# Expert results of a mixture-of-experts layer: weighted when they leave PSUM and added in DRAM to four sums per token, in place of six stored rows per token

## The reference

```python
router_logits = x @ gate_w.T
probs = softmax(router_logits)                   # 64 experts
topk_w, topk_idx = top_k(probs, 6)               # K = 6
topk_w = topk_w / sum(topk_w)
combine = sum(one_hot(topk_idx, 64) * topk_w)
h = silu(einsum('th,eih->tei', x, experts_w1))   # I = 176
y = einsum('tei,ehi->teh', h, experts_w2)
routed_out = einsum('teh,te->th', y, combine)
shared_out = (silu(g) * u) @ shared_down.T       # g, u from x @ shared_gate_up.T
x = layernorm(x + routed_out + shared_out)
```

## Time and profile before

| | |
|---|---|
| runs | 1177.99, 1176.19, 1179.95 us; median 1177.99 us |
| profiled execution | 1182.11 us; its span 1180.3 us |
| PE busy | 937.1 us (79%) |
| DVE busy | 787.1 us (67%) |
| POOL busy | 555.0 us (47%) |
| ACT busy | 414.3 us (35%) |
| DMA | 197.06 MB, mean 167 GB/s |
| router stage | 366 to 664 us, about 9.1 us a tile |
| expert stage | 669 to 1066 us, 6.75 us a unit |
| end stage | 1067 to 1172 us, about 3 us a tile |

### The profile page before, as it was taken

The page is one execution under the profiler, slowest core; times in us unless marked ns, Lnnn a source line. Parts: engine busy times, 40 slices in busy tenths (PEclk is TensorE's granted clock), DMA queues, the critical chain, the costliest instruction groups (busy, mean ns, idle before and its releaser), DMA issues.

```text
span 1180.3 us, 32353 instructions
## 1 busy us (share of the span) xinstructions
PE 937.1 (79%) x8988; PEld 806.4 (68%) x8988; DVE 787.1 (67%) x2416; ACT 414.3 (35%) x1061; POOL 555.0 (47%) x780
## 2 busy tenths in 40 slices
PE   5699999997988888888888399999999999980000
PEld 4577777775767888788877288888888888870000
DVE  5477777774435677767766566766676766746995
ACT  2355655553213443444343023232232232231121
POOL 1022222222003777777777345656656656663553
PEclk9899999998988999999999599999999999995555
DMA  7445555552311333333324366777777777727994
GB/s 237 127 144 184 175 168 167 182 180 65 89 58 43 107 104 104 106 106 106 105 92 155 100 202 207 223 233 216 229 215 231 232 231 221 230 97 263 305 301 140
DMA packets 136186, 197.06 MB, mean 167 GB/s; under 512 B 18398, under 2 KB 111063, under 8 KB 136153
## 3 DMA queue, kind: packets, MB, share of 16 engines
q1 hardware_dynamic: 68200, 104.04, 28.4%
q10 hardware_dynamic: 47920, 41.09, 12.3%
q0 software_dynamic: 20032, 51.55, 11.9%
HBM read 105.76 MB, written 95.03 MB: 170 GB/s over the span
## 4 chain that ended last, share of the span: by engine, by line
PE 64%; DVE 10%; issue 8%; ACT 5%; DMA 4%; POOL 4%; ACTq 2%; DVEq 1%; SPq 0%; POOLq 0%
PE psum L771 9%; PE psum L748 8%; PE psum L710 7%; PE psum L533 6%; PE psum L765 5%; PE psum L752 5%; PE psum L781 4%; DMA arena<-expert_results 3%; PE psum L588 3%; PE psum L522 3%; PE psum L676 3%; DVE arena L1158 2%; POOL pair_rs L1049 2%; PE psum L613 2%; PE psum L567 2%
## 5 line engine op out<-in xcount | busy, mean ns | idle before, releaser
L1084 POOL DMA_INDIRECT expert_results<-arena,udest x224 | 228.0, 1018 | 177.5 <-issue 146.3
L1066 POOL DMA_INDIRECT expert_rows<-row,dest x192 | 187.6, 977 | 69.0 <-issue 62.0
L1464 DVE COPY arena<-arena 128x896 f32 x224 | 130.3, 642 | 31.5 <-PE psum L752 28.5
L1037 POOL TENSOR_TENSOR xnb<-xn,c_bout 128x256 f32<-128x256 f32 x32 | 23.3, 728 | 201.7 <-DVE ln_r L1168 188.6
L771 PE MATMUL psum<-arena 128*128 128x128 f32 x896 | 115.5, 283 | 0.0
L771 PEld LDWEIGHTS psum<-arena 128*128 128x128 f32 x896 | 104.9, 193 | 9.7 <-issue 9.7
L748 PE MATMUL psum<-arena 128*128 128x256 f32 x448 | 110.4, 389 | 0.7 <-ACT arena L985 0.7
L976 ACT ACTIVATE arena<-psum 128x512 f32<-128x512 f32 x56 | 33.5, 598 | 206.7 <-PE psum L752 184.1
L1446 DVE COPY arena<-psum 128x512 f32<-128x512 f32 x112 | 72.2, 686 | 43.0 <-PE psum L781 40.4
L710 PE MATMUL psum<-x2t,c_sgu 128*128 128x128 f32 x768 | 92.8, 279 | 0.0
L710 PEld LDWEIGHTS psum<-x2t,c_sgu 128*128 128x128 f32 x768 | 89.9, 195 | 0.0
(11 more groups left out here) (205 smaller groups left out, 2017.5 us busy)
## 6 DMA issues: line engine op xcount, KB each, us to landing
expert_rows<-zeros SPq DMA_DIRECT2D x64, 536.0 KB, 4.8
arena<-expert_rows ACTq DMA_DIRECT2D x224, 134.0 KB
arena<-in_w_experts SPq DMA_DIRECT2D x64, 448.0 KB
arena<-expert_results SPq DMA_DIRECT2D x32, 768.0 KB, 5.5
xn<-in_x SPq DMA_DIRECT2D x32, 128.0 KB, 2.1
cbt<-in_ctx_t SPq DMA_DIRECT2D x32, 128.0 KB, 2.2
cn<-in_ctx SPq DMA_DIRECT2D x32, 128.0 KB, 2.1
xt<-in_x_t ACTq DMA_DIRECT2D x30, 128.0 KB, 4.6
```

What stands on the lines that cost most here:

```text
L1066: pool.indirect_dma_start(listd, bass.IndirectOffsetOnAxis(ap=dest[u][:, j:j + 1], axis=0), row[u][:], None).then_inc(sem(f"scatter{u}"), 16)
L1084: pool.indirect_dma_start(yd, bass.IndirectOffsetOnAxis(ap=udest[u][:, v:v + 1], axis=0), uy[:, 4 * u + v, :], None, bounds_check=T * K - ...
L1464: dve.tensor_copy(uw[:, 4 * u + v, :], ring[:, bass.ds(e & (WS - 1), 1), :].rearrange("p a n -> p (a n)"))\
```

## The change

The weights are normalised in the router stage, tile by tile: DVE takes a reciprocal (`weight_sum`) and ACT writes the six weights into the token's row (`row_weights`), ahead of the scatter, which now waits for them. The row has 272 floats: features, six expert numbers, six weights, the token's number, three zeros. `c_places` and the two instructions at the end of the tables are gone.

In the expert stage a block's weight for each of its rows comes from a compare and a multiply with the row's expert numbers and weights (`block_share`, `block_weight`). `y_evac` has one activation for each block, four instead of two, with that weight as the scale. The destination is the token's number, or for a row that no token fills (weight 0) a row of its own past the 4096 (`block_token`, `block_taken`, `block_dest`). The result goes to `expert_sums`: four tensors of 4096 + 128 rows, where block v of each unit is added to sum v by an indirect DMA with `compute_op=add`. An add may not meet another add to the same row in flight, so the add of block v in unit q waits until that of block v in unit q-1 has landed (`added`; semaphores `sum0` to `sum3`). All 128 rows of each block are now written. SP clears the sums, 33 DMAs of 512 KB, in the router stage (`clear_sums`).

In the end stage a tile's load is four pieces of 1 KB for each token (128 x 4 x 256), and DVE has four plain additions (`add_part`) in place of six weighted ones.

The core of the diff:

```diff
+SUMS = 4
+        def added(q, v):
+            return sem(f"sum{v % SUMS}"), 16 * (EACH * q + v // SUMS + 1 + PRIMED)
...
+            def clear_sums(k, u):
+                sp.dma_start(sums_by_tile[:, rows(4 * k + u), :].rearrange("a p n -> p a n"), zeros[:, 0:SUMS, 0:D])\
+                  .then_inc(sem("sums_cleared"), 16)
...
-                load(sp, y6[u].rearrange("p k n -> p (k n)"),
-                     yd.rearrange("(t k) n -> t (k n)", k=K)[rows(t), :], f"y6_ld{u}")
+                load(sp, parts[u], sums_by_tile[:, rows(t), :].rearrange("a p n -> p a n"), f"part_ld{u}")
...
+            def row_weights(k, u):
+                t = 4 * k + u
+                act.wait_ge(*ev("winv_done", t))
+                act.activation(row[u][:, D + K:D + 2 * K], wexp[u % 2][:], ACT.Copy, scale=winv[u % 2][:, 0:1])\
+                   .then_inc(sem("weights_done"), 1)
...
             def y_evac(k, u):
-                act.wait_ge(*ev("y_ready", 2 * k + u))
-                act.wait_ge(sem(f"y_out{u}"), 64 * k + 16)
-                act.activation(uy[:, 4 * u:4 * u + 2, :], ps_uy[:, 0:2, :], ACT.Copy)
-                act.activation(uy[:, 4 * u + 2:4 * u + 4, :], ps_uy[:, 2:4, :], ACT.Copy).then_inc(sem("y_evac"), 1)
+                q = 2 * k + u
+                act.wait_ge(*ev("y_ready", q))
+                act.wait_ge(*ev("uweight_done", q))
+                for v in range(4):
+                    act.wait_ge(*added(q - 2, v))
+                    m = act.activation(uy[:, 4 * u + v, :], ps_uy[:, v, :], ACT.Copy, scale=uweight[u][:, v:v + 1])
+                m.then_inc(sem("y_evac"), 1)
...
+                pool.wait_ge(*ev("weights_done", t))
...
-            def scatter_result(k, u):
+            def add_result(k, u):
                 q = 2 * k + u
                 pool.wait_ge(*ev("udest_done", q))
                 pool.wait_ge(*quad("y_evac", q))
-                settle(pool)
                 for v in range(4):
-                    pool.indirect_dma_start(yd, bass.IndirectOffsetOnAxis(ap=udest[u][:, v:v + 1], axis=0), uy[:, 4 * u + v, :],
-                                            None, bounds_check=T * K - 1, oob_is_err=False).then_inc(sem(f"y_out{u}"), 16)
+                    pool.wait_ge(*added(q - (v < SUMS), (v - SUMS) % 4))
+                    settle(pool)
+                    pool.indirect_dma_start(sums, bass.IndirectOffsetOnAxis(ap=udest[u][:, v:v + 1], axis=0), uy[:, 4 * u + v, :],
+                                            None, compute_op=ALU.add).then_inc(sem(f"sum{v % SUMS}"), 16)
...
-            def place_sum(k, u):
+            def block_weight(k, u):
                 q = 2 * k + u
-                dve.wait_ge(*ev("uplace_done", q))
-                dve.wait_ge(*ev("udest_done", q - 2))
-                dve.tensor_reduce(uplace_s[u][:], uplace[:], AX, ALU.add).then_inc(sem("uplaces_done"), 1)
+                dve.wait_ge(*ev("ushare_done", q))
+                dve.wait_ge(*quad("y_evac", q - 2))
+                dve.tensor_reduce(uweight[u][:], ushare[:], AX, ALU.add).then_inc(sem("uweight_done"), 1)
...
+            def block_dest(k, u):
+                q = 2 * k + u
+                dve.wait_ge(*ev("utaken_done", q))
+                for v in range(4):
+                    dve.wait_ge(*added(q - 2, v))
+                settle(dve)
+                dve.tensor_tensor(udest[u][:], utaken[u][:], aside[:], ALU.add).then_inc(sem("udest_done"), 1)
...
-            quads(dve, [(2, ux_evac), (1, place_mul), (1, place_sum), (1, copy_weights), (2, place_int)],
-                  (copy_weights, place_mul), packed)
+            quads(dve, [(2, ux_evac), (1, block_share), (1, block_token), (1, block_weight), (1, copy_weights),
+                        (1, block_taken), (2, block_dest)], (copy_weights, block_share), packed)
...
-                    dve.scalar_tensor_tensor(r[:], y6[u][:, j, :], weights[:, bass.ds(t, 1), j:j + 1]
-                                             .rearrange("p a k -> p (a k)"), r[:] if j else slot(xall, t),
-                                             ALU.mult, ALU.add)\
+                    dve.tensor_tensor(r[:], parts[u][:, j, :], r[:] if j else slot(xall, t), ALU.add)\
...
-            tiles(dve, [(2, sums3), (0, add_slot(0)), (1, add_slot(3)), (2, mean3), (0, add_slot(1)), (1, add_slot(4)),
-                        (0, add_slot(2)), (1, add_slot(5))], ways=4)
+            tiles(dve, [(2, sums3), (0, add_part(0)), (1, add_part(2)), (2, mean3), (0, add_part(1)), (1, add_part(3))],
+                  ways=4)
```

109 lines of the change are left out of this document (66 added, 43 removed).

## The result

The change makes the kernel slower: 1234.27 us (median of 4 runs, 1227.34 to 1242.23) against 1178.97 us (4 runs, 1176.19 to 1181.24), a ratio of 1.047 with a 95% interval of 1.040 to 1.054. The prediction said 1163, range 1143 to 1200. The profiled execution of after took 1227.34 us, the shortest of its four; its span is 1225.4. All ratios in this document are of fast runs alone, while medians and ranges take in a slow run where a kernel had one: of the adds of 64 floats that is the profiled run itself, and of the plain writes on the second kind of chip one of four.

A forecast was written before the change was run, and what follows sets the result against it. TensorE was taken to bound the expert stage, DVE and its loads the end stage. Terms -27 (end stage), -0.75 (tables), +1 (router), +10 (expert stage), +2 (drain) gave -15 us: median 1178 to 1163, range 1143 to 1200.

The forecast's parts named there:

- What bounds the kernel: Whole kernel: TensorE holds the expert stage (busy 348.75 of 350 us); DVE and its loads together hold the end stage.
- End stage: Final additions: a tile falls to 2.2 us by DMA bandwidth, a gain of 27 us, with ends of 34 and 6.
- Tables and router stage: Before the experts: two table instructions go, 0.75 us gained; one more wait on POOL costs 1 us (0 to 4).
- First loop: Expert stage: weights wait for `y_evac`, delaying `ux_evac` and `b_up`; 3 us over 56 units, 0 to 14.
- Second loop: Expert stage: `udest` waits for landed adds; 2.7 us used of 2.16 us of room, costing 10 us over 56 units.
- Writing the descriptors of an add: Expert stage, POOL: a second source might cost something for each of four adds; 0.4 us in all (0 to 1.2).
- The landing: Expert stage: an add reads its DRAM row before writing, so it lands 0.8 us later; the other end doubles 2.3 us.
- POOL's own pace: Expert stage: POOL needs 5.7 us of 6.75 a unit, 7.0 with added costs; nearly bound, giving the same 10 us.
- Rival 1: Expert stage: adds land 2 us later or descriptors take 0.3 us longer; unit 7.7 us, about 1206 us; chance 0.18.
- Rival 3: Expert stage: adds fill the DMA engines, share about 1.0; unit 7.2 us, 24 us more, total 1177; chance 0.12.
- Rival 2: Expert stage: POOL is shut out during all DVE weight copies, 2.3 us instead of 0.5; 1197 us; chance 0.06.
- bound of 76 us of extra time: Expert stage, second loop's upper end: 6.2 us used, 4.1 over the room, 76 us; the range kept only 45 us.

The follow-up runs named there:

- adds of 64 floats: Changed kernel adding only 64 of each row's 256 floats, into a narrow tensor, with as many descriptors: 1212.36 us, ratio 1.023 to the kernel before.
- plain writes: Changed kernel with plain writes instead of adds, all waits kept: 1159.08 us, ratio 0.981; on a chip where the kernel before took 1448.17 us, 1369.22 us, 0.944.
- experiments with one load at a time: Changed kernel with four adds of 64 floats (1212.36 us), or with two adds of 512 floats (1198.19 us; with eight sums 1190.95 us).

## Why the prediction was wrong, point by point

- **What bounds the kernel** was read rightly: TensorE in the expert stage, DVE and loads at the end. The plain writes, with TensorE at 342 of 350 us, show that all the change's other work did fit under it, but for 9 us.
- **End stage**: -27 forecast, -25.0 measured; 2.27 us a tile for 2.2. The value by bandwidth was the right choice. The share is 0.93 at 294 GB/s.
- **Tables and router stage**: right, within 2 us; POOL's scatters of two tiles are still 9.07 us apart.
- **First loop**: `y_evac` was forecast at 1.65 us and takes 1.57. Its wait is in the traces and costs little: plain writes, which keep it and all other new waits, have a unit of 6.92 us against 6.76, 9 us over 56 units, inside the 0 to 14.
- **Second loop, the step that failed: "Writing the descriptors of an add: no row shows it. [...] I take 0.4 (0 to 1.2)."** The guess was for all four. An add's instruction takes 1.555 us in place of 0.985, which is 2.3 us for four: six times the guess and nearly twice its upper end. With 0.30 us between two, POOL needs 7.4 us a unit, and 7.6 with the longer ones beside DVE's copies, where the forecast had 5.7 to 7.0. That alone puts POOL in TensorE's place: 7.97 us a unit with a quarter of the bytes, and 54 to 58 us back when the count is halved.
- **The landing** was forecast 0.8 us longer (0 to 2.3). From the last add to `udest` it is 4.47 us and was 3.36, both medians; 0.57 of the difference is the descriptor, 0.5 comes behind it. So this guess held. With the measured sizes of these two terms and the forecast's for the others, 0.57 + 0.5 + 0.35 + 2.3 + 0.5 + 0.1 = 4.3 us are used of 2.16 us of room, 2.2 over, 0.7 a unit: 7.5 us by the loop alone.
- **POOL's own pace** was called "nearly bound" at 7.0 us, with the same guess of 0.4 in it. With the measured size it is the tighter of the two: 4 x (1.608 + 0.30) = 7.6 us, with 0.49 of waits for `y_evac` and for adds on top the measured 8.12. It needs no landing and no phase, and should have led. The DMA engines are as near to their end (0.94 of 8.12 us is 7.6 as well), so that in after itself two bounds lie side by side; the experiments with one load at a time tell them apart.
- **Rival 1** is what happened in direction, and its own condition ("its descriptors take 0.3 us longer") was passed by another 0.27; it gave 1206 and a chance of 0.18. Its other condition, a landing 2 us longer, did not come about.
- **Rival 3** was true as well, and the forecast's sum had no term for it: the share rose to 0.94 and the bytes cost 32 to 44 us once POOL is out of the way. Its price, 24 us, was too low since it counted bytes. Counting engine time, q0 took 0.242 x 1225 - 0.130 x 1158 = 146 us more of all sixteen engines than with plain writes, 2.6 us a unit; with the 0.71 x 6.75 = 4.8 of before that is 7.4 us a unit for full engines, 7.9 at 0.94, an estimate, against 8.12 measured.
- **Rival 2** is refuted as it was priced: no add waited out the four copies, which go on for 2.42 us. Of 52 adds of after that ran beside copies for nearly all their length, 25 took under 1.65 us and the others up to 2.00, so 0.45 us is the most that the copies cost one. The rule of the Trainium skill ("SBUF — State Buffer", section "SBUF: two separate sides"), that the descriptors cannot be written while such a copy runs, is neither shown nor refuted by this: one copy takes 0.61 us or more, and a delay of up to 0.45 us is also what waiting for the end of one copy would give. What the prediction made of it, all four copies in one, is what was wrong.
- On the other rule of the Trainium skill ("Collectives: The Full Stack", section "The bandwidth ceiling"), that a DMA which adds has half the rate of a copy: the trace agrees in direction and shows more: 0.97 us of all sixteen engines for an add against 0.34 for a write of the same rows, 2.9 times and not twice. It deserved more than the place beside a rival.
- The **range** ended at 1200 because the dearer half of rival 1 was cut off. Two unknown costs on a resource that is 84% used (5.7 of 6.75 us) should have kept the bound of 76 us of extra time that the text itself had worked out; the time came within 6 us of what that end gives (1178 - 27 - 0.75 + 1 + 2 + 76 = 1229). That it came so near is luck: that end has 1.2 us for the descriptors and 2.3 for the landing, where 2.3 and 0.5 were measured. The other end of the same loop was given as 1.2 us used, but its terms at their least add up to 0.1; both lie within the room, so nothing hangs on it.
- **The clock** had no term. In the forecast TensorE never waits for long; in after it did, and 0.40 us a unit of TensorE's work went to the lower level.
